# Gate stage of a fused attention and quantised FFN kernel: GpSimd rounds two rows and multiplies two more tiles

## The reference

```python
def _act_fake_quant(x, clip_factor):
    scale = jax.nn.sigmoid(clip_factor) * jnp.max(jnp.abs(x)) / QMAX
    return jnp.clip(_ste_round(x / scale), -QMAX - 1.0, QMAX) * scale
...
xq = _act_fake_quant(x, clip_x[0])
gate = jnp.einsum('bsh,ih->bsi', xq, _weight_fake_quant(w_gate))
up = jnp.einsum('bsh,ih->bsi', xq, _weight_fake_quant(w_up))
h = _act_fake_quant(jax.nn.silu(gate) * up, clip_down[0])
return jnp.einsum('bsi,hi->bsh', h, _weight_fake_quant(w_down))
```

## Time and profile before

| | us |
|---|---|
| median of 3 runs | 275.73 |
| lowest, highest | 275.56, 279.0 |
| the profiled execution | 275.67 |
| its span, first to last instruction | 273.9 |
| TensorE busy in the span | 254.1 |
| VectorE busy | 226.4 |
| ScalarE busy | 183.3 |
| GpSimd busy | 145.9 |

### The profile page before, as it was taken

How to read it: one execution, slowest core, us unless ns; L and a number is a source line. 1 busy time by engine, 2 the same in 40 slices (tenths; PEclk the granted TensorE clock), 3 DMA queues, 4 the chain that set the end, 5 groups by cost and what they waited for, 6 DMA issues and landing times.

```text
span 273.9 us, 8463 instructions
## 1 busy us (share of the span) xinstructions
PE 254.1 (93%) x3529; PEld 174.6 (64%) x3529; DVE 226.4 (83%) x483; ACT 183.3 (67%) x325; POOL 145.9 (53%) x144
## 2 busy tenths in 40 slices
PE   5799999989799799989999999998989999998994
PEld 5568788679578677957977977875634434443331
DVE  4879678499779958995996876888888999999994
ACT  5796463562369557858768358437699999838991
POOL 6998693871790395069169233005012779850570
PEclk9999999999999999999999999999999999999999
DMA  5991306204400800390291142040009489000277
GB/s 161 347 276 42 117 2 222 91 0 175 138 2 2 278 33 2 122 244 6 56 288 26 33 146 39 9 149 6 0 34 183 114 221 366 7 0 0 80 257 279
DMA packets 30310, 31.20 MB, mean 114 GB/s; under 512 B 12928, under 2 KB 20672, under 8 KB 30272
## 3 DMA queue, kind: packets, MB, share of 16 engines
q1 hardware_dynamic: 30272, 30.66, 37.4%
HBM read 19.48 MB, written 8.42 MB: 102 GB/s over the span
## 4 chain that ended last, share of the span: by engine, by line
PE 53%; DVE 26%; ACT 12%; issue 5%; DMA 1%; POOL 1%; DVEq 0%; ACTq 0%
PE psum L901 10%; PE psum L1290 6%; DVE arena L1461 5%; PE psum L941 4%; PE psum L1309 3%; PE psum L926 3%; PE psum L1062 3%; ACT silu L864 2%; PE psum L1008 2%; PE psum L1068 2%; PE psum L1063 2%; PE psum L1064 2%; PE psum L1069 2%; ACT silu L846 2%; PE psum L1051 2%
## 5 line engine op out<-in xcount | busy, mean ns | idle before, releaser
L1461 DVE TENSOR_TENSOR arena<-psum,xq_mem 128x512 f32<-128x512 f32 x64 | 39.6, 681 | 3.8 <-PE psum L926 3.7
L560 POOL TENSOR_TENSOR xT_lo<-arena,xT 128x512 fp32r<-128x512 f32 x14 | 17.5, 1273 | 45.4 <-ACT xT L689 45.4
L1290 PE MATMUL psum<-xq_mem,guT 128*128 128x512 bf16 x152 | 33.9, 379 | 0.2
L1290 PEld LDWEIGHTS psum<-xq_mem,guT 128*128 128x128 bf16 x152 | 14.3, 98 | 19.4 <-DVE arena L1675 1.8
L1686 DVE TENSOR_REDUCE h_max<-arena 128x1 f32<-128x1024 f32 (+1 forms) x24 | 25.9, 1123 | 0.2
L846 ACT ACTIVATE silu<-psum,gu_x 128x1024 f32<-128x1024 f32 (+1 forms) x24 | 24.4, 1026 | 2.1 <-PE psum L1290 1.1
L689 ACT ACTIVATE xT<-arena 128x512 fp32r<-128x512 f32 x14 | 8.1, 623 | 22.6 <-PE psum L901 20.9
L941 PE MATMUL psum<-arena 64*32 64x128 f32 x1024 | 19.4, 274 | 1.5 <-DVE arena L1461 1.5
L671 ACT ACTIVATE arena<-psum,pmask 128x512 f32<-128x512 f32 x32 | 20.2, 684 | 0.4 <-PE psum L1069 0.4
L1309 PE MATMUL psum<-arena,dT 128*128 128x512 bf16 x80 | 18.9, 380 | 1.2 <-DVE arena L1745 0.6
L926 PE MATMUL psum<-arena 32*64 32x128 f32 x1024 | 19.7, 278 | 0.1
(11 more groups left out here) (247 smaller groups left out, 721.4 us busy)
## 6 DMA issues: line engine op xcount, KB each, us to landing
arena<-in_x SPq DMA_DIRECT2D x9, 512.0 KB, 3.8
x_dram<-arena SPq DMA_DIRECT2D x8, 512.0 KB, 4.0
pooled<-x_dram SPq DMA_DIRECT2D x8, 512.0 KB, 5.3
out<-pooled SPq DMA_DIRECT2D x15, 256.0 KB, 2.1
xin<-in_x_t SPq DMA_DIRECT2D x7, 512.0 KB, 4.4
cs_rows<-cs_dram SPq DMA_DIRECT2D x12, 256.0 KB, 5.3
pooled<-in_w_qkv_t SPq DMA_DIRECT2D x3, 256.0 KB, 5.0
pooled<-in_w_down SPq DMA_DIRECT2D x1, 704.0 KB, 7.8
```

The costliest lines, as they stand in the source:

```text
L560: pool.tensor_tensor(xT_lo[:, k, :], xrotT[:, k, :], xT[:, k, :].bitcast(F32), ALU.subtract).then_inc(xl_ok, 1)
L1290: mm = pe.matmul(in_order(o[:, 512 * half:512 * half + 512], 2 * n + half), gT[i][:, v, c, :], xq_rows(2 * n + half, c), start=(c == 0), s ...
L1461: dve.tensor_tensor(dec[:, c, r, :, :], bank[S_BANK[r]].rearrange("q (n k) -> q n k", n=PP), two_heads, ALU.mult).then_inc(dec_done, 1)
```

## The change

ScalarE no longer rounds rows 5 and 6; GpSimd rounds them itself in its queue with a tensor_scalar (f32 in, int8 out) from the same scale, ahead of widening them. Steps (0, 2) and (1, 1) become lent: ScalarE copies their up tile, GpSimd multiplies, and VectorE's products of them are gone. VectorE's reductions are put in another order in the first two blocks. Widening 4 and 5 now stand ahead of step (0, 2) in GpSimd's queue, and widening 7 ahead of step (1, 5) instead of (1, 4).

```diff
-LENT = ((4,), (2, 5), (0, 1, 3, 4, 5), (1, 3, 5))
-ACT_ROWS = {(0, 0): 3, (0, 1): 4, (0, 3): 5, (1, 0): 6, (1, 4): 7}
+LENT = ((2, 4), (1, 2, 5), (0, 1, 3, 4, 5), (1, 3, 5))
+ACT_ROWS = {(0, 0): 3, (0, 1): 4, (1, 4): 7}
...
-POOL_ROWS = {(0, 0): 3, (0, 3): 4, (0, 5): 5, (1, 1): 6, (1, 4): 7}
+POOL_ROWS = {(0, 0): (3,), (0, 2): (4, 5), (1, 1): (6,), (1, 5): (7,)}
+POOL_ROUNDS = (5, 6)
...
+            def round_rows(i, k):
+                pool.wait_ge(q8_ok, i - 1)
+                pool.wait_ge(xq_ok, i - 3)
+                pool.tensor_scalar(q8[:, k, :], pooled_b[:, i, :], x_sc[:, 4:5], None, ALU.mult).then_inc(q8_ok, 1)
+
             def widen_rows(i, k):
...
-                    if (n, v) in POOL_ROWS:
-                        widen_rows(POOL_ROWS[n, v], POOL_ROWS[n, v] % 2)
+                    for i in POOL_ROWS.get((n, v), ()):
+                        if i in POOL_ROUNDS:
+                            round_rows(i, i % 2)
+                        widen_rows(i, i % 2)
...
             product(0, 0)
             product(0, 1)
             largest(0, 0)
-            product(0, 2)
+            largest(0, 1)
             product(0, 3)
             largest(0, 3)
-            largest(0, 2)
             product(0, 5)
             dve.wait_ge(x1_out, 16 * G)
+            largest(0, 2)
             product(1, 0)
             largest(1, 0)
-            product(1, 1)
+            largest(0, 5)
             largest(0, 4)
-            largest(0, 1)
             product(1, 3)
-            largest(0, 5)
             product(1, 4)
             largest(1, 3)
             largest(1, 1)
```

## The result

| | before | after |
|---|---|---|
| median, us | 275.65 | 279.08 |
| lowest, us | 275.56 | 278.86 |
| profiled span, us | 273.9 | 277.2 |
| last reduction of the stage ends (from the span's start) | 246.29 | 249.57 |

The medians lie 3.4 us apart; the ratio is 1.0144, with an interval of 1.0111 to 1.0177. That is slower by less than 2%, as the prediction's largest chance had it, but 0.9 us beyond the end of its range (278.2) and 3.2 us beyond its likeliest time.

The account below looks back on a forecast made before the run. TensorE's stream and VectorE's queue were taken to set the gate stage's end. With a 1.1 us rounding, VectorE's freed 2.26 us became silu waits and the queues summed to +0.2: 275.67 + 0.2 = 275.9 us, range 275.1 to 278.2.

Parts of the forecast that it names:

- the prediction's largest chance: Whole kernel: time stays within two per cent (5.5 us) of before; chance 0.96.
- What bounds the kernel: Gate stage: TensorE's stream and VectorE's queue both set its end, so a gain needs both to move; TensorE about 1.6 us.
- ScalarE's and VectorE's terms: Gate stage: ScalarE loses two roundings and gains two copies, net -0.28 us; VectorE loses two products, 2.26 us.
- GpSimd's rounding: GpSimd's queue in the gate stage: one tensor_scalar of 1024 columns takes 1.1 us, range 1.04 to 2.36.
- the prediction's own rule: Both roundings precede a multiplication a silu tile waits for: +0.9 us at 1.6, each further us of rounding counts twice.
- The waits: First two blocks: silu (0,5) waits 0.9 us and (1,1) 0.7 for GpSimd; TensorE 0.52 in (0,5), 0.41 in (1,2).
- rival 2: Slow GpSimd rounding: at 2.36 us silu (0,5) waits 2.2, (1,4) 0.9 more, TensorE in (1,1); 278.2 us; chance 0.22.
- the forecast's R: Time of one rounding on GpSimd, taken as 1.1 us.
- One stall that was to vanish: TensorE's weight loads waiting for VectorE's product (1,4) at 222.75: the 0.63 us (0.38 in the layout) was to go.
- Rival 3: VectorE's freed 2.26 us reach TensorE and the stage's end: 274.1 us; needs a rounding under 0.4; chance 0.12.
- Rival 4: VectorE slows GpSimd by 0.13 us on each instruction in the gate stage: 277.3 us; chance 0.04.
- The late rows: Rows 6 and 7, widened later (217.3 and 223.5), cost nothing; row 7 lands by 229.4, 2.2 us to spare.

Follow-up runs that it names:

- round_only: Kernel before, with its lent steps and VectorE's order kept, but roundings 5 and 6 moved to GpSimd: 275.66 us, 0.0 against before.
- lend_only: Changed kernel with roundings 5 and 6 given back to ScalarE, widening 5 moved behind multiplication (0,4), steps (0,2) and (1,1) still lent: 276.19 us.
- short_round: Changed kernel with GpSimd rounding only the first 384 of 1024 columns of rows 5 and 6: 276.00 us.

## Why the prediction was wrong

**What bounds the kernel: right, as far as the runs go.** The stage's end is set twice in the changed kernel too: the filler ends at 249.76, the last reduction at 249.57. Relieving ScalarE alone (round_only) gained nothing. Relieving VectorE alone wasn't tried: lend_only takes two products from it but gives ScalarE two copies.

**ScalarE's and VectorE's terms: right.** -0.28 us for ScalarE and -2.26 for VectorE were forecast; their busy times in the stretches above add up to 0.26 and 2.10 less than before. What VectorE was freed of became waits, as said.

**GpSimd's rounding: this is the step that failed.** "From above by the two-input multiplication, 2.36" was no bound. It rested on the thought that an instruction with one input can't be dearer than one with two, and nothing in the trace of before showed that. The value taken, 1.1, was worse founded still: affine selects of 64 and 128 columns, another operation, stretched to 1024 through a slope of 0.06 us. The trace of before also had dearer selects of the same 64x64 shape, which the prediction left aside:

```profile
L505 POOL TENSOR_SCALAR_AFFINE_SELECT xq_mem<-xq_mem 64x64 f32<-64x64 f32 x2 | 0.9, 470 | 0.1
```

With 0.234 to 0.470 us for one shape, a difference of 0.06 us between two shapes carries no slope. The term measured 2.85. Put in, the prediction's own rule (0.9 at 1.6, and 2 us for each us above it) gives 0.9 + 2 x 1.25 = 3.4, and 3.3 to 3.4 was measured.

The estimate from the Trainium skill (GPSIMD Engine Reference, section 3.1), 1.54 us from 1.8 cycles an element, was nearer but short as well: 2.54 ns a column are 3.0 cycles at the 1.2 GHz that the page gives. The same page's section 4.1 calls GpSimd's one-input operations roughly line rate; the cast keeps to that here (1.04 us for 1024 columns), the tensor_scalar doesn't.

**The waits: right in place and kind, but for one stall.** Silu (0,5), (1,1) and (1,4) on GpSimd, TensorE in (1,1) and (1,2): as rival 2 had them, with 2.60 and 1.29 for its 2.2 and 0.9. Near the forecast's R (short_round, 1.26) the kernel came to 276.00, where the forecast said 275.9 for 1.1. One stall that was to vanish is still there: TensorE's weight loads wait 0.64 us for product (1,4) at 225.62, before 0.63 at 222.75, since silu (1,4) comes late. In short_round it is gone, so this too comes with R.

**Rival 3 (faster): didn't come;** its condition, a rounding under 0.4 us, wasn't near. **Rival 4 (VectorE holding GpSimd up): didn't come.** GpSimd's multiplications and widenings took 2.36 and 1.04 as before. **The late rows: right that they cost nothing.** Widening 7 ended at 226.45, 3 us behind the forecast's 223.5, with the fourth block at 234.8, and no wait for a transposed row shows.

**The chances.** 0.22 on a slow rounding was too little for a price that no row showed, and the range's end stood on a bound that was none: with R open to 3.9, which rival 2 itself named as the point where 2% is passed, it should have gone further.

## What to carry to other kernels

An operation that the trace doesn't hold is bounded only by rows of the same operation; a neighbour with more inputs is no upper bound, and where the layout says that each us of it counts twice, the range has to stay open there. Before work is moved to the idle engine, ask whose buffer its queue frees: GpSimd had 13.7 us of room in the stage, but round_only shows that the two roundings, 5.7 us, already fill what stood ahead of (0,4) and (1,2). Two moves that each fit into the room may not fit together.

## What the runs showed of the hardware

On GpSimd a tensor_scalar with one multiplication takes 0.27 us + 2.54 ns a column of f32 on 128 partitions (1.26 us for 384 columns, 1.57 for 512, 2.05 for 704, 2.85 for 1024), whatever the output type (int8, bf16, f32) and nearly whatever the scalar; a tensor_tensor of two full inputs took 2.36 us for 1024 columns, with one operand repeated 1.90, and a cast from f32 to int8 or bf16 1.04.
